# Swiglu blocks of a fused four-layer transformer kernel: rounded halves of first-layer weights and of activations on the scalar engine, remainders one unit later

## What is computed

```python
def _swiglu_ffn(x, w1, w2):          # x 896 x 256, w1 256 x 2048, w2 1024 x 256
    h = x @ w1
    x_glu, x_lin = jnp.split(h, 2, axis=-1)
    x_glu = jnp.minimum(x_glu, LIMIT)             # 7
    x_lin = jnp.clip(x_lin, -LIMIT, LIMIT)
    g = x_glu * jax.nn.sigmoid(ALPHA * x_glu) * (x_lin + 1.0)    # 1.702
    return g @ w2
...
y = _rmsnorm(latents, s2)
latents = latents + _swiglu_ffn(y, w1_1, w2_1)
```

## Time and profile before

| | |
|---|---|
| median of 3 runs | 2322.79 us (2315.61 to 2324.64) |
| the profiled execution | 2322.28 us, span 2320.4 us |
| busy, share of the span | PE 86%, PEld 63%, DVE 70%, ACT 38%, POOL 36% |
| chain that ended last | PE 60%, DVE 23%, issue 10%, ACT 3%, POOL 2% |
| casts L1377 in all MLPs | 208, 133.7 us busy |
| remainders L1378 | 208, 186.0 us busy |
| POOL L1559 in all MLPs | 104, 106.5 us busy |

### The profile page before, as it was taken

The page is one execution under the profiler, slowest core; times in us unless marked ns, Lnnn a source line. Parts: engine busy times, 40 slices in busy tenths (PEclk is TensorE's granted clock), DMA queues, the critical chain, the costliest instruction groups (busy, mean ns, idle before and its releaser), DMA issues.

```text
span 2320.4 us, 35838 instructions
## 1 busy us (share of the span) xinstructions
PE 2002.0 (86%) x11112; PEld 1464.4 (63%) x11112; DVE 1619.0 (70%) x3586; ACT 891.3 (38%) x2427; POOL 830.1 (36%) x950
## 2 busy tenths in 40 slices
PE   5879997999996877999888999685886968898878
PEld 4657776889895656777665555473444745565557
DVE  5856767677776876666665676595775958777765
ACT  4545553222222643555424444222331234444421
POOL 2235554666662233555420010041000424444433
PEclk9989998999997988999889999896997979999979
DMA  4100000211101000000100010101001000000100
GB/s 176 33 14 15 13 0 1 101 73 37 52 41 68 1 1 7 15 25 31 59 7 14 14 61 0 45 1 55 0 0 65 1 1 11 20 10 10 64 1 16
DMA packets 21631, 67.18 MB, mean 29 GB/s; under 512 B 880, under 2 KB 18568, under 8 KB 18832
## 3 DMA queue, kind: packets, MB, share of 16 engines
q1 hardware_dynamic: 21520, 65.78, 8.0%
HBM read 64.83 MB, written 0.95 MB: 28 GB/s over the span
## 4 chain that ended last, share of the span: by engine, by line
PE 60%; DVE 23%; issue 10%; ACT 3%; POOL 2%; DMA 1%; DVEq 0%; SPq 0%; POOLq 0%; ACTq 0%
PE ps L809 11%; PE ps L848 9%; PE ps L683 9%; PE ps L643 5%; PE ps L648 4%; PE ps L746 4%; PE ps L696 4%; PE ps L728 3%; PE ps L678 3%; POOL arena L1530 2%; PE ps L723 2%; PE ps L635 2%; DVE g_split_sb L1378 2%; DVE arena L1240 1%; DVE arena L1432 1%
## 5 line engine op out<-in xcount | busy, mean ns | idle before, releaser
L1530 POOL TENSOR_TENSOR arena<-arena,rinv 112x375 f32<-112x375 f32 (+1 forms) x448 | 372.0, 830 | 579.6 <-DVE rinv L1248 571.8
L683 PE MATMUL ps<-arena 128*112 128x375 f32 (+1 forms) x1280 | 387.5, 410 | 20.0 <-ACT arena L975 13.2
L809 PE MATMUL ps<-h_split_sb,w_split_sb 128*128 128x448 f32 x1536 | 355.5, 376 | 5.3 <-DVE h_split_sb L1368 4.3
L1559 POOL TENSOR_TENSOR w_split_sb<-wml,ones 128x256 fp32r<-128x256 f32 (+1 forms) x104 | 106.5, 1024 | 608.0 <-PE ps L809 396.6
L809 PEld LDWEIGHTS ps<-h_split_sb,w_split_sb 128*128 128x128 f32 x1536 | 298.4, 195 | 33.5 <-issue 5.9
L696 PEld LDWEIGHTS ps<-cst,arena 112*125 112x125 f32 (+1 forms) x1408 | 216.1, 183 | 156.5 <-POOL arena L1530 56.7
L848 PE MATMUL ps<-g_split_sb,w_split_sb 128*128 128x448 f32 x1248 | 292.9, 372 | 21.5 <-DVE g_split_sb L1378 21.1
L1243 DVE TENSOR_REDUCE negmax<-ps 112x1 f32<-112x375 f32 (+1 forms) x288 | 159.3, 553 | 159.2 <-PE ps L683 158.8
L848 PEld LDWEIGHTS ps<-g_split_sb,w_split_sb 128*128 128x128 f32 x1248 | 232.7, 189 | 55.6 <-DVE g_split_sb L1378 36.8
L975 ACT ACTIVATE arena<-ps,negmax 112x375 f32<-112x375 f32 (+1 forms) x384 | 190.5, 501 | 190.3 <-DVE negmax L1243 189.4
L696 PE MATMUL ps<-cst,arena 112*125 112x112 f32 (+1 forms) x1408 | 229.5, 275 | 38.6 <-POOL arena L1530 38.2
(11 more groups left out here) (159 smaller groups left out, 3014.1 us busy)
## 6 DMA issues: line engine op xcount, KB each, us to landing
wml<-in_wm_L_moe SPq DMA_DIRECT2D x8, 2052.0 KB, 8.2
craw<-in_ctx SPq DMA_DIRECT2D x40, 375.0 KB
wml<-in_wm_L_m SPq DMA_DIRECT2D x3, 3072.0 KB, 14.0
wat<-in_wa_L_ca SPq DMA_DIRECT2D x2, 2560.0 KB, 9.4
wml<-in_wm_L_m SPq DMA_DIRECT2D x2, 2048.0 KB, 9.7
arena<-gates_hbm SPq DMA_DIRECT2D x1, 3584.0 KB, 11.0
wat<-in_wa_L_sa SPq DMA_DIRECT2D x1, 2560.0 KB, 8.8
wat<-in_wa_L_sa SPq DMA_DIRECT2D x2, 1024.0 KB, 9.6
```

Source lines behind the costliest of these rows:

```text
L683: last = mm(ps[0:S, S_BANK + s % blk.s_banks, i * blk.nk:(i + 1) * blk.nk], qz[:, parity(b), head_of(u) if blk.dh == 16 else u], kT[:, par ...
L809: last = mm(out, w[:, k2, v], h_split_sb[:, h, k2, tokens], start=k2 == 0 and i == 0, stop=k2 == DC - 1 and i == 2)
L1530: pool.tensor_tensor(p3, p3, r3, ALU.mult).then_inc(scaled, 1)
```

## The change

In the Swiglu blocks alone:

- ACT rounds the first-layer weights, as a Copy in fp32r: chunk 0 ahead of the block's first instruction on ACT (behind all of ACT's work of the attention before), chunk f + 1 behind the sigmoid of unit 2f. POOL no longer does L1559 there; it waits for w1_rounded and subtracts. Second-layer weights stay as they were.
- ACT rounds g32 of unit t - 1 between the linear half and the sigmoid of unit t, once DVE has made it (g_made) and down of unit t - 3 has read the buffer (g_used); the last unit's follows its own sigmoid.
- DVE no longer casts. The remainder of unit t - 1 is taken in unit t, between the multiply and the product, after a wait for g_rounded. DVE's product raises g_made and DVE goes on without waiting for it.
- The semaphore w_rounded is cut in three (w_rounded, w1_rounded, w2_rounded), for the other blocks with the same meaning.

```diff
+                def round_weights(f):
+
+                    if f == 0:
+                        act.wait_ge(wml_loaded[0], 16 * (wml_count[n][0] + 1))
+                    w = mlp_weights(n)[0].rearrange("p k (v n) -> p k v n", v=2)[:, :, :, f * P:(f + 1) * P]
+                    go(chunk_parts(f, 2)[0], w, ACT.Copy).then_inc(w1_rounded, 1)
+
+                def round_hidden(t, unit):
+
+                    act.wait_ge(g_made, st["clip"] + t + 1)
+                    if unit - st["ff"] >= 2:
+                        act.wait_ge(g_used, unit - 1)
+                    go(g_split_sb[:, t % 2, 0], g32[:, t % 2], ACT.Copy).then_inc(g_rounded, 1)
+
+                if blk.act == "swiglu":
+                    round_weights(0)
                 for b2_ in range(B // 2):
                     keep_tokens(b2_)
...
                             go(tc[:, t % 2], ps[:, 2 * (t % 2) + 1, 0:HALF], ACT.Identity, bias=1.0).then_inc(f_lin, 1)
+                            if t:
+                                round_hidden(t - 1, unit - 1)
                             act.wait_ge(f_min, st["clip"] + t + 1)
                             go(tb[:, t % 2], ta[:, t % 2], ACT.Sigmoid, scale=1.702).then_inc(f_act, 1)
+                        if blk.act == "swiglu" and t % 2 == 0 and f + 1 < FC:
+                            round_weights(f + 1)
+                        if blk.act == "swiglu" and t == 2 * FC - 1:
+                            round_hidden(t, unit)
...
                 def split_hidden(t, unit):
 
-                    if unit - st["ff"] >= 2:
-                        dve.wait_ge(g_used, unit - 1)
-                    link(v.tensor_copy(g_split_sb[:, t % 2, 0], g32[:, t % 2]))
+                    if blk.act == "swiglu":
+                        dve.wait_ge(g_rounded, st["clip"] + t + 1)
+                    else:
+                        if unit - st["ff"] >= 2:
+                            dve.wait_ge(g_used, unit - 1)
+                        link(v.tensor_copy(g_split_sb[:, t % 2, 0], g32[:, t % 2]))
...
                             link(v.tensor_tensor(tc[:, t % 2], tc[:, t % 2], ta[:, t % 2], ALU.mult))
+                            if t:
+                                split_hidden(t - 1, unit - 1)
                             dve.wait_ge(f_act, unit + 1)
-                            link(v.tensor_tensor(g32[:, t % 2], tc[:, t % 2], tb[:, t % 2], ALU.mult))
-                        split_hidden(t, unit)
+                            v.tensor_tensor(g32[:, t % 2], tc[:, t % 2], tb[:, t % 2], ALU.mult).then_inc(g_made, 1)
+                        if blk.act != "swiglu" or t == 2 * FC - 1:
+                            split_hidden(t, unit)
...
-                    pool.tensor_tensor(hi, w, one, ALU.mult).then_inc(w_rounded, 1)
-                    pool.wait_ge(w_rounded, 2 * chunk + 1)
+                    if BLOCKS[n].act == "swiglu":
+                        pool.wait_ge(w1_rounded, st["clip"] // 2 + f + 1)
+                    else:
...
                     pool.tensor_tensor(lo, w, hi.bitcast(F32), ALU.subtract).then_inc(w1_split, 1)
```

More of the change, by code:

```diff
@@ L373, in build @@
         inverted = sem("inverted")
-        w_rounded = sem("w_rounded")
+        w_rounded, w1_rounded, w2_rounded = sem("w_rounded"), sem("w1_rounded"), sem("w2_rounded")
+        g_made, g_rounded = sem("g_made"), sem("g_rounded")
         w1_split, w2_split, h_split = sem("w1_split"), sem("w2_split"), sem("h_split")
@@ L1556, in split_weights @@
                     wait(pool, f_full, unit - 2)
-                    one = ones[:, 0:1].unsqueeze(1).unsqueeze(1).broadcast_to([P, DC, width, P])
-                    pool.tensor_tensor(hi, w, one, ALU.mult).then_inc(w_rounded, 1)
-                    pool.wait_ge(w_rounded, 2 * chunk + 1)
+                    if BLOCKS[n].act == "swiglu":
+                        pool.wait_ge(w1_rounded, st["clip"] // 2 + f + 1)
+                    else:
+                        one = ones[:, 0:1].unsqueeze(1).unsqueeze(1).broadcast_to([P, DC, width, P])
+                        pool.tensor_tensor(hi, w, one, ALU.mult).then_inc(w_rounded, 1)
+                        pool.wait_ge(w_rounded, chunk - st["clip"] // 2 + 1)
                     pool.tensor_tensor(lo, w, hi.bitcast(F32), ALU.subtract).then_inc(w1_split, 1)
@@ L1564, in split_weights @@
                     wait(pool, g_used, unit - 2)
-                    pool.tensor_tensor(hi, w2[:, f], ones[:, 0:1].broadcast_to([P, D]), ALU.mult).then_inc(w_rounded, 1)
-                    pool.wait_ge(w_rounded, 2 * chunk + 2)
+                    pool.tensor_tensor(hi, w2[:, f], ones[:, 0:1].broadcast_to([P, D]), ALU.mult).then_inc(w2_rounded, 1)
+                    pool.wait_ge(w2_rounded, chunk + 1)
                     pool.tensor_tensor(lo, w2[:, f], hi.bitcast(F32), ALU.subtract).then_inc(w2_split, 1)
```

## The result

| | before | after |
|---|---|---|
| median of 20 runs each, same chip | 2316.68 us (2309.83 to 2324.64) | 2304.23 us (2297.11 to 2315.01) |
| ratio to before, 95% interval | | 0.9945 [0.9932, 0.9958] |
| second comparison, another chip (11 and 6 runs) | 2319.09 us | 2300.76 us, 0.9917 [0.9896, 0.9938] |
| span of the profiled executions | 2320.4, 2312.8 us | 2301.8, 2299.4 us |

A forecast was written before the change was run, and what follows sets the result against it. DVE, with its waits for POOL, was taken to set the pace in the Swiglu blocks. 13.0 us from both blocks plus 3.65 from the attentions made 16.65, giving 2306 us; range 2299 to 2316.

The forecast's parts named there:

- (a): DVE in the Swiglu blocks: without the cast and the wait after the product, its own work is 5.38 us a pair.
- (b): POOL in the Swiglu blocks: its three remaining operations a chunk cost DVE 2.15 us a pair (bounds 0 to 2.61).
- (c): Pair of units: DVE needs 7.53 us, PE 7.30; the pair falls from 8.47 to 7.55.
- rival 2: Swiglu blocks: waits for POOL shrink with its work, PE becomes the bound at 7.30 us a pair; 2301 us, chance 0.11.
- (d): ACT's added copies: 0.58 us a unit and 0.66 a pair, no table load, not the bound, new waits cost nothing.
- Rival 1: DVE waits 0.5 us a unit for ACT, pair stays 8.47; 2320.6 us, chance 0.19 including what lies between it and forecast.
- (e): First-layer weights: ready with 1.1 us of cover, except chunk 1 at block start, whose ups start 2.0 us later.
- Rival 4: First-layer weights come late: at 7.0 us for their chain the pair takes 9.4 us; 2332 us, slower, chance 0.06.
- (f): Whole Swiglu block: last down ends at 1562.2 instead of 1568.7, at full clock; gain 6.5 us a block, 13.0 for both.
- rival 3: PE's clock falls at the new stall between ups of units 1 and 2; 2.5 us a block, 2311 us, chance 0.12.
- (g): Attentions before the blocks: POOL no longer holds DVE up; L2_ca gains 1.35 us net, L2_sa 2.3, together 3.65 (0 to 5).
- Other blocks: only the numbering of semaphores changes: Blocks other than Swiglu: nothing but semaphore numbers changes, so no time was forecast for L3_ca (0).

The follow-up runs named there:

- weights_alone: The changed kernel with the rounding of the activations back on DVE in its old place; 2307.12 us, 0.9941 of the kernel before.
- no_clip: The changed kernel without DVE's clip of the linear half in the Swiglu units; 2302.84 us in one run.
- chunks_late: The changed kernel, but POOL rounds first-layer weights of chunks 0 and 1 itself, after the attention's last weighing; 2295.01 us, 0.9884 of the kernel before.
- tail_late: The changed kernel with ACT's rounding of chunk 0, and so POOL's first operations, behind the attention's last weighing; 2303.43 us, 0.9929 of the kernel before.

## Why the prediction came out right

Median and gain are close to the forecast (16.65 us, against 12.7 by the first ratio and some 19 by the second), but by errors in both directions. By the steps:

- **(a)** held. The five operations that are left of a unit take 5.38 a pair without POOL (7.32 less the measured 1.94); minimum, clip and multiply take 0.54, 0.41 and 0.66 = 1.61 from start to start.
- **(b)** 2.15 was taken near the top of its range, 1.94 measured: 1.10 for the subtract (1.15 forecast), 0.84 for the two short ones (1.00). The rule of the Trainium skill (SBUF — State Buffer, "Who interferes with whom") that such operations exclude each other is borne out: the product lasts 1.72 while POOL's subtract of 1.33 runs. But the loss is not a price for each POOL operation: 1.28 for the same three in `weights_alone`.
- **(c)** is where the block was mis-sized: 7.30, not 7.55, which was DVE's 5.38 + 2.15; with 1.94 for POOL it would have come to 7.32. It is rival 2's pace, with DVE needing as much as PE to within 0.02 us, and `no_clip` shows PE to be the floor. 0.25 us over some five pairs is the 1.3 us by which L2_m1 beat the forecast (7.83 against 6.5).
- **(d)** held: 0.57 (forecast 0.58) and 0.62 (0.66), no table load, no wait for them on DVE, ACT 48% busy. The copies cost less than their length on ACT, since the next operation starts 0.47 after the first kind. Rival 1 did not occur.
- **(e)** held to 0.1 us: idle 1.99 (2.0) at the start, none later. Rival 4 did not occur in after; in `weights_alone` PE did wait 0.19 us a pair for POOL's subtract.
- **(f)** held in all but the pairs: full clock at the end, last down 1.49. The clock did not fall at the new stall (ups of 2.70 behind it), so rival 3 did not occur at its place.
- **(g)** was right in its mechanisms and wrong in its sum. The batch of 33.71 in L2_ca went to 31.06, the chain of L2_sa to 7.67, and the additions of the tail grew by 1.3, each within 0.1 of the working. But L2_sa gained 8.76 instead of 2.3 and L2_ca lost 2.95 instead of gaining 1.35. What the sum lacked goes, as far as the rows show, with the granted clock (0.78 against 0.73 in L2_sa's first stretch, half clock in L2_ca's last weighing). I had put a price on the clock only at the two places in the block.
- **"Other blocks: only the numbering of semaphores changes"** is the step that failed outright. The list of what the change removes has an item more, the place of everything behind in DVE's program. In its place the runs showed two gaps of DVE of some 4.2 us in L3_ca in all ten traces without the cast, worth 4.0 us over four batches by the means of fourteen traces. The 5.65 of these two pairs of profiles is not all theirs. The rows ahead of the prediction could not give the size, but the loop was in the code.

In all: blocks 15.3 (13.0 forecast), L2_sa 8.8 (2.3), L2_ca -2.95 (+1.35), L3_ca -5.65 (0), sum 15.5. That the total is near is luck in good part: 8.8 us more than forecast in the blocks and L2_sa, and 10 less in L2_ca and L3_ca.

## What to carry to other kernels

When a second engine is close behind the one that sets the pace, look for the pace of that second engine first: PE's 7.30 us could be read from another stage and is what the pair came to, and it made two edits worth less together than apart. Follow work of POOL that is moved off one stage to where it lands; behind the last weighing no operation of DVE was stretched (`chunks_late`: the reciprocal 2.96 and the multiply 0.62 as elsewhere), and that gave the fastest version. After any edit that changes the length of an engine's program, look in the profile for idle time released by "issue" in loops that the edit did not touch, and compare stages, not spans.

## What the runs showed of the hardware

- A loop of DVE that had run for three turns without a gap (0.3 us from the branch back to its first instruction) got one of 4.2 to 4.9 us at both branches back once 60 instructions ahead of it were gone, with five loads of instructions to a turn: ten traces against four.
- The idle time just before does not decide PE's clock: the same matmuls after the same 3.05 us of idle PE took 2.48 us in before, 3.98 in `chunks_late` and 4.75 in `tail_late`, and 1.99 us of idle in after brought no fall. The Trainium skill (TensorE: Matmul & The Clock Gate, "The HAM clock gate") says that idleness brings the half rate back; which idleness counted here was not isolated.
- Removing DVE work can remove DVE's waits for POOL with it: without the 0.4 us of clip a unit, the loss fell from 1.94 to 0.35 + 0.53 = 0.88 us a pair (0.97 and 1.15 against 0.62).
- An ACT Copy from SBUF into fp32r took 0.57 us for 128x448 and 0.62 for 128x512, between sigmoids and without a table load.
